# The scalar chain of three layer norms with one operand of each VectorE operation in PSUM

## What is computed

```python
def _layernorm(x, axis=-1, eps=1e-05):
    m = jnp.mean(x, axis=axis, keepdims=True)
    v = jnp.var(x, axis=axis, keepdims=True)
    return (x - m) / jnp.sqrt(v + eps)

x = x + attn(_layernorm(x), Wqkv, bqkv, Wo, bo)          # one head of 256
x = x + fake_quant(_layernorm(x)) @ fake_quant(ctx)      # q = clip(round(x / s + z), 0, 255)
x = x + ffn(_layernorm(x), c1_w, c2_w, w1, w2t)          # in each block of 64 hidden units only the
                                                         # one with the largest rank-16 score is kept
```

## Time and profile before

| | |
|---|---|
| three timed runs | 858.01, 853.85, 857.35 us (median 857.35) |
| profiled execution | 854.2 us, span of the instructions 852.4 us |
| PE busy | 816.6 us, 96% of the span, granted clock 1.00 throughout |
| DVE busy | 524.0 us (61%) |
| ACT busy | 232.7 us (27%) |
| POOL busy | 251.4 us (29%) |
| chain that ended last | PE 81%, DVE 15%, ACT 1%, DMA 1% of the span |

### The profile page before, as it was taken

The page is one execution under the profiler, slowest core; times in us unless marked ns, Lnnn a source line. Parts: engine busy times, 40 slices in busy tenths (PEclk is TensorE's granted clock), DMA queues, the critical chain, the costliest instruction groups (busy, mean ns, idle before and its releaser), DMA issues.

```text
span 852.4 us, 10818 instructions
## 1 busy us (share of the span) xinstructions
PE 816.6 (96%) x3932; PEld 658.4 (77%) x3932; DVE 524.0 (61%) x812; ACT 232.7 (27%) x324; POOL 251.4 (29%) x120
## 2 busy tenths in 40 slices
PE   4999997889899999999999999999999999999998
PEld 4888975447678788878888888878887888778886
DVE  4855799999967852577237832784258624882222
ACT  5366535763320132012201221023102120123100
POOL 2844388515520233013401142024201340124100
PEclk9999999999999999999999999999999999999999
DMA  9126401001210123001210121011200220002022
GB/s 338 38 85 210 151 1 53 1 13 63 99 50 12 32 69 99 12 25 61 87 36 0 49 98 49 12 49 54 93 12 25 74 98 0 25 26 97 0 99 99
DMA packets 16791, 53.20 MB, mean 62 GB/s; under 512 B 3200, under 2 KB 3456, under 8 KB 16640
## 3 DMA queue, kind: packets, MB, share of 16 engines
q1 hardware_dynamic: 16624, 51.85, 17.9%
q10 hardware_dynamic: 144, 1.05, 0.3%
HBM read 48.70 MB, written 4.19 MB: 62 GB/s over the span
## 4 chain that ended last, share of the span: by engine, by line
PE 81%; DVE 15%; ACT 1%; DMA 1%; issue 1%; POOL 0%; SPq 0%; DVEq 0%
PE bank L1187 14%; PE bank L1189 14%; PE bank L1188 14%; PE bank L1368 12%; PE bank L1370 12%; PE bank L1369 12%; DVE stats L797 2%; PE bank L1344 1%; DVE x L910 1%; PE bank L1333 1%; DVE xT_lo L823 1%; DVE pick L960 1%; DVE xn L889 1%; DMA W_raw<-wqkv 1%; DVE cand L953 1%; DVE pairs L1051 1%
## 5 line engine op out<-in xcount | busy, mean ns | idle before, releaser
L471 POOL TENSOR_TENSOR w_lo<-w_raw,w_hi 128x1024 fp32r<-128x1024 f32 x56 | 141.1, 2535 | 471.2 <-ACT w_hi L600 471.2
L1368 PE MATMUL bank<-w_hi,h_hi 128*128 128x512 f32 x448 | 177.6, 396 | 0.0
L1187 PE MATMUL bank<-xT_hi,w_hi 128*128 128x512 f32 x448 | 175.8, 392 | 0.0
L1370 PE MATMUL bank<-w_hi,h_lo 128*128 128x512 f32 x448 | 174.7, 390 | 0.0
L1369 PE MATMUL bank<-w_lo,h_hi 128*128 128x512 f32 x448 | 174.6, 390 | 0.0
L1189 PE MATMUL bank<-xT_hi,w_lo 128*128 128x512 f32 x448 | 174.5, 390 | 0.0
L1188 PE MATMUL bank<-xT_lo,w_hi 128*128 128x512 f32 x448 | 174.5, 389 | 0.0
L968 DVE SCALAR_TENSOR_TENSOR bank<-bank,maskT 128x512 f32<-128x512 f32 x56 | 39.0, 699 | 154.5 <-PE bank L1189 153.3
L983 DVE TENSOR_TENSOR x<-bank,x 128x512 f32<-128x512 f32 x112 | 76.9, 688 | 76.4 <-PE bank L1370 75.0
L607 ACT ACTIVATE maskT<-bank 128x512 bf16<-128x512 bf16 x56 | 33.4, 597 | 290.8 <-PE bank L1344 290.8
L1370 PEld LDWEIGHTS bank<-w_hi,h_lo 128*128 128x128 f32 x448 | 84.1, 188 | 17.7
(11 more groups left out here) (140 smaller groups left out, 969.4 us busy)
## 6 DMA issues: line engine op xcount, KB each, us to landing
w_raw<-w SPq DMA_DIRECT2D x56, 512.0 KB, 3.3
x<-x_in SPq DMA_DIRECT2D x8, 512.0 KB, 10.5
ctx_raw<-ctx_in SPq DMA_DIRECT2D x8, 512.0 KB, 3.9
xn<-ctx_in SPq DMA_DIRECT2D x8, 512.0 KB, 4.8
out<-x SPq DMA_DIRECT2D x7, 512.0 KB, 2.6
W_raw<-wqkv SPq DMA_DIRECT2D x6, 512.0 KB, 10.4
c_raw<-c SPq DMA_DIRECT2D x56, 32.0 KB, 1.8
Wo_raw<-wo ACTq DMA_DIRECT2D x1, 1024.0 KB, 4.8
```

Of the source, the lines that this page charges most:

```text
L471: nc.gpsimd.tensor_tensor(lo, raw, hi.bitcast(F32), ALU.subtract).then_inc(w_lo_done, 1)
L1187: nc.tensor.matmul(dst, ah, bh, start=n == 0, stop=False)
L1368: nc.tensor.matmul(dst, h_hi[:, j, m], w2_hi[:, j, c], start=j == 0, stop=False)
L1370: last = nc.tensor.matmul(dst, h_lo[:, j, m], w2_hi[:, j, c], start=False, stop=j == GJ - 1)
```

## The change

`mv`, `newt` and three new names (`root`, `rstd_ps`, `nmr_ps`) become columns 0 to 47 of the score bank in PSUM. The root that ACT makes is now twice the standard deviation (scale 4 and 4 EPS). The Newton step is made on the root instead of on its reciprocal, root = sdev/4 + (var + EPS) * (1/sdev), and the reciprocal of that is the last step. The number of operations stays: five in a chain of rounds 0 and 2, seven in one of round 1. In round 1 `qmul` is now waited for before the shift is made, and the shift is made from it. Every two-tensor operation now has one input in SBUF and one in PSUM. No instruction changes place on any engine, and no other engine's instructions change but ACT's root, which reads PSUM.

```diff
-    mv = small("mv", [P, NT, 2], F32)
-    newt = small("newt", [P, NT], F32)
...
         score_bank = bank[6]
+
+        mv = score_bank[:, 0:2 * NT].rearrange("p (t m) -> p t m", m=2)
+        newt, root, rstd_ps, nmr_ps = (score_bank[:, (2 + i) * NT:(3 + i) * NT] for i in range(4))
...
                 nc.scalar.activation(sdev[:, s], mv[:, s, 1], ACT.Sqrt, bias=eps[:, 0:1],
-                                     scale=1.0).then_inc(sdev_ready, 1)
+                                     scale=4.0).then_inc(sdev_ready, 1)
...
                 link(nc.vector.reciprocal(rinv[:, s], sdev[:, s]))
-                link(nc.vector.scalar_tensor_tensor(newt[:, s], rinv[:, s], -0.5, rinv[:, s], ALU.mult, ALU.mult))
-                link(nc.vector.scalar_tensor_tensor(newt[:, s], var, EPS, newt[:, s], ALU.add, ALU.mult))
-                link(nc.vector.scalar_tensor_tensor(rstd[:, s], newt[:, s], 1.5, rinv[:, s], ALU.add, ALU.mult))
-                ins = nc.vector.scalar_tensor_tensor(nmr[:, s], mean, -1.0, rstd[:, s], ALU.mult, ALU.mult)
+                link(nc.vector.scalar_tensor_tensor(newt[:, s], var, EPS, rinv[:, s], ALU.add, ALU.mult))
+                link(nc.vector.scalar_tensor_tensor(root[:, s], sdev[:, s], 0.25, newt[:, s], ALU.mult, ALU.add))
                 if rnd == 1:
-                    link(ins)
-                    nc.vector.tensor_scalar(qmul[:, s], rstd[:, s], inv1, None, ALU.mult)
-                    ins = nc.vector.tensor_scalar(qadd[:, s], nmr[:, s], inv1, qp[:, 1:2], ALU.mult, ALU.add)
-                ins.then_inc(rstd_ready, 1)
+                    link(nc.vector.reciprocal(rstd_ps[:, s], root[:, s]))
+                    link(nc.vector.tensor_scalar(qmul[:, s], rstd_ps[:, s], inv1, None, ALU.mult))
+                    link(nc.vector.scalar_tensor_tensor(nmr_ps[:, s], mean, -1.0, qmul[:, s], ALU.mult, ALU.mult))
+                    nc.vector.tensor_scalar(qadd[:, s], nmr_ps[:, s], qp[:, 1:2], None,
+                                            ALU.add).then_inc(rstd_ready, 1)
+                else:
+                    link(nc.vector.reciprocal(rstd[:, s], root[:, s]))
+                    nc.vector.scalar_tensor_tensor(nmr[:, s], mean, -1.0, rstd[:, s], ALU.mult,
+                                                   ALU.mult).then_inc(rstd_ready, 1)
...
-            nc.vector.memset(eps[:, :], EPS).then_inc(eps_ready, 1)
+            nc.vector.memset(eps[:, :], 4 * EPS).then_inc(eps_ready, 1)
```

## The result

The changed kernel takes 849.26 us (median of 9 runs, 846.39 to 851.22), the kernel before, on the same chip, 854.36 us (9 runs, 852.14 to 858.01). The ratio is 0.9933, with a 95% interval of 0.9916 to 0.9950: 5.7 us less, between 4.3 and 7.2. A second comparison later gave 0.9937 (0.9913 to 0.9960). The profiled execution took 849.98 us.

A forecast was written before the change was run, and what follows sets the result against it. PE, busy 816.6 of 852.4 us, was taken to bound the kernel, with DVE setting the pace from 129 to 245 us. Stalls -5.56 and longer chains +0.24 made -5.3, from 855.9 to 850.6 us; range 846.8 to 855.4.

The forecast's parts named there:

- the PSUM cost: Tiny DVE operations reading PSUM, 30 in DVE's stretch: -0.3 to +3.6 us in all, taken as 0.
- the chain at 134 us: DVE's `rstd` at 134.28 us stalls behind POOL's addition: 2.01 less 0.16, gain 1.85 us.
- the new chain of round 1: The shift now waits for `qmul`, `qadd` gets shorter: net 0.08 us lost, three times, 0.24 us.
- The chain at 158 us: DVE's `newt` at 158.45 us stalls behind POOL's additions: 2.13 less 0.16, gain 1.97 us.
- PE's wait: First chain, up to 42 us: DVE done some 6.2 us earlier, but PE waits only 1.74 us, so gain 1.74.
- the 3.6 us that DVE was to need less: Sign of success: from 129 to 245 us, where DVE sets the pace, it needs 3.6 us less.
- The term of 0: PSUM operands in the chains put at 0 us, since 512-column rows from PSUM and SBUF differ by next to nothing.
- The reading of the stalls: DVE operations with two SBUF inputs and SBUF output stand still until POOL's running operation ends; one-input reciprocals do not.
- The race at the first rounding: Rival, 0.20: at 138 us POOL starts before DVE's first rounding, which waits some 2.1 us; 852.7 us.
- That PSUM operands cost: Rival, 0.09: 0.08 to 0.12 us in each of 30 operations cuts the gain to 1.7 to 2.9; 853.6 us.
- that nothing is gained: Rival, 0.08: a single SBUF access stalls, or saved time meets POOL's next operation; sum near 0, 855.9 us.
- the upper executions of before are those with more stalls: Rival, 0.12: slower executions lose one or two more chain operations to POOL; the change brings all to 848.9 us.

The follow-up runs named there:

- e8: Changed kernel with ACT's root and round 1's rstd in PSUM, as mean and variance, the chain's other outputs in SBUF; 0.9950 of the kernel before.
- e2: Changed kernel with the chain's PSUM operands kept in round 0 alone, SBUF in rounds 1 and 2; 0.9977 of the kernel before.
- e4: Kernel before, old arithmetic, with one PSUM input in two-tensor chain operations except the first (rinv times rinv); 0.9972 of the kernel before.
- 7: Changed kernel with mean, variance and ACT's root in PSUM, all that DVE's chain writes in SBUF; 0.9960 of the kernel before.
- e6: Kernel before with POOL's additions x += bo replaced by setting the whole tile to zero (writes SBUF, reads nothing); 851.47 us, one run.
- e1: Changed kernel's new arithmetic with mean, variance and all intermediates back in SBUF in every round; 1.0018 of the kernel before, 854.67 us.
- e3: Changed kernel with the chain's PSUM operands kept in round 1 alone, SBUF in rounds 0 and 2; 0.9953 of the kernel before.

## Why the prediction was right

**The total.** 850.6 us was forecast, 849.26 measured, in the range. I took 5.3 us off; the medians on one chip differ by 5.1, the ratio gives 5.7. The 1.3 us between forecast and result come from the starting point: I took 5.3 off 855.9, the mean of four executions, which is 1.5 above the median of nine, 854.36. The top of the range has a slip, since I had put the upper end of the PSUM cost at 3.6 us and added 3.0; it should have been 856.0.

**The stalls.** Of the terms, the chain at 134 us gave 1.77 us (DVE's next work -3.05, its start -1.28), which is 1.85 less the 0.08 for the new chain of round 1. The chain at 149 us, which had no stall, lost 0.10 (1.29 to 1.39), those of round 2 0.02 (0.86 to 0.88). The chain at 158 us gave 1.85 (-4.24 against -2.39), and 1.97 less 0.08, or 1.89, was the forecast. The first gave PE's wait: of its shift at 43 us, -1.12, the late start hides 0.75, so it was worth 1.87. That is slightly over 1.74, for PE starts a product 0.23 us after the one before it though each is listed with 0.39. I had said the transpose would start near 41.5; it was 42.14, 41.4 without the late start. The first chain's gain did carry through to 129 us (-1.28), and no part came back in the last stage (-4.24 at 161 us, -4.2 at the end). Of the 3.6 us that DVE was to need less from 129 to 245 us, 3.4 came (-1.28 at the stage's start, -4.66 at the pick at 236.72 us).

**PSUM operands.** The term of 0 was right within 0.1 us, and the bound of 3.6 us far off. (The 512-column rows give -11 to -1 ns, not "-11 to +1".) A three-operand form with a PSUM input takes 166 to 169 ns with its output in PSUM too and 158 with it in SBUF, where both in SBUF took 160; the last reciprocal of a chain takes 171 to 190 ns, where e8 with both places in SBUF has 166 to 178, so 13 ns at most; ACT's root from PSUM takes 262 ns against 295. The 65 ns that the Trainium skill ("VectorE: DVE Perf Modes", the TRN2 errata) gives for PSUM are not seen in any of these rows.

**The reading of the stalls.** It was right for operations with two tensors, and incomplete for those with one. I took the reciprocal as the sample of "one input". But the earlier trace rows held the counterexample: the rounding has one tensor, from SBUF to SBUF, and I wrote myself that POOL slows it. `qmul` and `qadd` are of its form. The change happened to put their inputs in PSUM as well, so the sum was right; the runs e2 (1.80 us), e4 (1.60), 7 (1.83) and 8 (1.38) show what it would have cost otherwise. The Trainium skill says so: by "SBUF — State Buffer", section "Who interferes with whom", `tensor_scalar` can enter a mode that holds the pair shared with GpSimd, and an instruction with two SBUF inputs contends with a GpSimd instruction that reads SBUF, not with one that only writes it. The first agrees with these four stalls, though no run here shows the mode itself; the second agrees with e6.

**The rivals.** The race at the first rounding was run and won again, by the same 0.05 us: 135.19 against 135.24 on POOL (138.24 and 138.29 before). The stage did move as one piece. The sum of the eight roundings stayed near 10.6 us in the changed kernel. That PSUM operands cost, and that nothing is gained, fell with the rows above. That the upper executions of before are those with more stalls is not borne out: the changed kernel has a spread too, 846.4 to 851.2 us.

**The spread.** I could not say what the 4 us between executions are. The two traces of the kernel with later pairs show it for one pair, since they differ by 6.3 us in the span (843.6 and 849.9). 3.14 us are there at the transposes at 18.07 us already: the first weights land after 6.61 us in one and 7.63 in the other, and PE's first products run at the higher level of its clock in one (0.28 us) and at the lower in the other (0.41). The rest begins with a race between DVE and POOL in `pick_first`, on which the shift of 3.12 us bears. DVE's sixth pick in the two executions, then POOL in the slower one:

```profile
225.38 0.69 DVE L964 TENSOR_TENSOR pick<-cand,cmax 128x512 bf16<-128x512 bf16 x1
```
```profile
228.50 2.73 DVE L964 TENSOR_TENSOR pick<-cand,cmax 128x512 bf16<-128x512 bf16 x1
```
```profile
228.30 2.38 POOL L472 TENSOR_TENSOR w_lo<-w_raw,w_hi 128x1024 fp32r<-128x1024 f32 x1 [2.89 <-ACT w_hi L601]
```

In the slower one POOL's lo part of a weight starts 0.20 us ahead of it, and the pick takes 2.0 us more; 1.5 us of it reach PE (shift 4.66 us). Right behind it PE's granted clock falls to 0.50, a product of 512 columns takes 0.63 us instead of 0.39, and the shift grows to 6.7 us. The clock shows in the times as well: of the 29 executions of the kernel before beside e1 to e4, the four with a mean granted clock of 1.000 average 852.3 us, the five with 0.995 or less 855.1. It isn't all, since those four alone run from 851.2 to 853.3 us.

## What to carry to other kernels

Where a tiny VectorE operation lasts 2 us, look for a GpSimd operation that reads SBUF and ends with it; here each such stall had one. Give every such operation, with two tensors or of the `tensor_scalar` form, one input in PSUM, for there the price was 13 ns at most for the tiny ones; leave none out, since the stall moves to the first that is left. Price the saving by the wait of the engine that bounds, not by the time that VectorE gets back: 6.2 us on DVE were worth 1.74.

## What the runs showed of the hardware that I had not expected

- With one SBUF tensor, the form decides: the chains' reciprocals took 0.19 us at most in every run, beside POOL's additions too, `tensor_scalar` up to 1.83 us.
- POOL writing SBUF without reading it stops none of them (four operations at 0.16 us).
- PE's granted clock fell to 0.62 for the stretch from 146.0 to 150.5 us, after an idle time of 1.95 us, and sixteen products took 5.29 us instead of 3.62. In the second trace of the changed kernel it fell at the same products (5.30 us); in the kernel before, where PE idles there as well (2.30 us), and in the one with later pairs (2.28 and 2.27), it stayed at the higher level. e1 and e3 show 0.89 from 105 to 120 us instead. What decides it was not settled.
- What such a fall costs differs. In the first trace of the changed kernel it took some 0.5 us, because DVE then found 0.40 us of idle time; in the second, with the same slow products, DVE had none, and from the chain at 147 us to the next one it took 6.26 us, where the first took 6.70 and e3, without the fall, 6.19. The clock falls once more in both traces, at 228 and at 227 us (0.50 at its lowest); in the first DVE lost nothing by it, its shift against the kernel before is -4.18 at 229.43 us and -4.68 at 232.75.
